# Degree sums on GpSimd, counts turned by DMA in the second gate layer, and a last product in halves, in a four-layer graph network on one core

## The reference, cut to what matters

```python
# layer 0: x1 = x @ W1 + b1, then four gate layers, on the edge list of a fixed graph (row, col)
deg = segment_sum(ones, col);  dis = maximum(deg, 1.0) ** (-0.5)
alpha = tanh(x_i @ gw[:512] + x_j @ gw[512:] + gb)
gnn_out = gnn_out + segment_sum(dis[row] * dis[col] * alpha * x_j, col)
# layer 1: two mean layers
mean = segment_sum(h[src], dst) / maximum(deg, 1.0)
h = h @ W_self + mean @ W_neigh + b
# layer 2: attention, summed over src instead of dst
e = exp(-leaky_relu(al[src] + ar[dst]));  h_prime = segment_sum(e * h[dst], src) / (rowsum + 1e-5)
# layer 3: GCN
out = relu(segment_sum((x @ W)[src] * dinv[src] * dinv[dst], dst) + b)
x = layernorm(x + out)
```

## Time and profile before

| what | us |
|---|---|
| median of 3 runs | 1544.73 (1543.46 to 1545.18) |
| profiled execution | 1543.31, its span 1541.5 |
| PE busy | 1516.2 (98%) |
| DVE busy | 880.5 (57%) |
| ACT busy | 751.4 (49%) |
| POOL busy | 189.9 (12%) |
| granted TensorE clock | 0.998 |

### The profile page before, as it was taken

One profiled execution on the slowest core, in us unless ns is written; L12 is line 12 of the kernel. 1 busy time (PEld: TensorE's weight loads), 2 busy tenths in 40 slices (PEclk: granted clock), 3 DMA queues, 4 the chain that ended last, 5 costly groups with the idle time before them and its releaser, 6 DMA issues.

```text
span 1541.5 us, 19211 instructions
## 1 busy us (share of the span) xinstructions
PE 1516.2 (98%) x6965; PEld 1217.6 (79%) x6965; DVE 880.5 (57%) x1401; ACT 751.4 (49%) x1358; POOL 189.9 (12%) x315
## 2 busy tenths in 40 slices
PE   7999999999999999999999999999999999999997
PEld 5877877878887888788878777888788778877775
DVE  8878888887645353322333344567598356435346
ACT  7567677768733332334332133335696246533232
POOL 1110021324200000000000000212053013100013
PEclk9999999999999999999999999999999999999999
DMA  5333153325774434433344424564466248545245
GB/s 193 118 111 123 34 185 131 101 83 191 262 258 145 155 107 134 141 100 134 114 167 128 147 80 155 193 215 162 149 193 192 94 143 295 183 131 171 91 126 180
DMA packets 103198, 231.75 MB, mean 150 GB/s; under 512 B 23162, under 2 KB 25972, under 8 KB 103096
## 3 DMA queue, kind: packets, MB, share of 16 engines
q1 hardware_dynamic: 89996, 191.54, 39.1%
q10 hardware_dynamic: 13100, 38.86, 6.5%
HBM read 170.98 MB, written 59.37 MB: 149 GB/s over the span
## 4 chain that ended last, share of the span: by engine, by line
PE 92%; DVE 4%; ACT 3%; issue 1%; DMA 0%; POOL 0%; DVEq 0%; POOLq 0%; ACTq 0%
PE bank L980 17%; PE bank L836 15%; PE bank L838 15%; PE bank L837 15%; PE bank L991 9%; PE bank L984 8%; PE bank L982 7%; PE bank L1044 2%; ACT Tt L1125 2%; PE bank L906 1%; DVE Tt L1433 1%; PE bank L874 1%; DVE oK L1708 1%; DVE Zl L1474 0%; ACT Zh L1159 0%
## 5 line engine op out<-in xcount | busy, mean ns | idle before, releaser
L836 PE MATMUL bank<-wh,xh 128*125 128x512 f32 x1032 | 415.3, 402 | 0.4 <-issue 0.4
L837 PE MATMUL bank<-wl,xh 128*125 128x512 f32 x1040 | 410.4, 395 | 0.0
L838 PE MATMUL bank<-wh,xl 128*125 128x512 f32 x1040 | 409.5, 394 | 0.0
L980 PE MATMUL bank<-Zh,Mh 125*125 125x512 f32 x1000 | 399.6, 400 | 1.0 <-ACT Mh L1107 1.0
L1407 DVE TENSOR_TENSOR xl<-xs,xh 128x1000 fp32r<-128x1000 f32 x130 | 155.4, 1198 | 291.5 <-ACT xh L1090 291.2
L1090 ACT CAST xh<-xs 128x1000 fp32r<-128x1000 f32 x130 | 132.9, 1026 | 304.5 <-PE bank L838 292.9
L991 PE MATMUL bank<-Zl,Mh 125*125 125x512 f32 x600 | 236.6, 394 | 0.0
L838 PEld LDWEIGHTS bank<-wh,xl 128*125 128x125 f32 x1040 | 193.0, 186 | 48.9
L837 PEld LDWEIGHTS bank<-wl,xh 128*125 128x125 f32 x1040 | 193.1, 186 | 44.4
L836 PEld LDWEIGHTS bank<-wh,xh 128*125 128x125 f32 x1032 | 191.1, 185 | 45.2 <-issue 0.7
L980 PEld LDWEIGHTS bank<-Zh,Mh 125*125 125x125 f32 x1000 | 185.4, 185 | 46.2 <-ACT Mh L1107 1.1
(11 more groups left out here) (171 smaller groups left out, 1811.7 us busy)
## 6 DMA issues: line engine op xcount, KB each, us to landing
xs<-xT_d SPq DMA_DIRECT2D x80, 500.0 KB, 3.6
Ar<-a_d SPq DMA_DIRECT2D x100, 312.5 KB, 3.3
xs<-hT_d SPq DMA_DIRECT2D x40, 500.0 KB, 3.5
x_d<-XO ACTq DMA_DIRECT2D x30, 512.0 KB, 4.9
R<-x_d SPq DMA_DIRECT2D x60, 256.0 KB, 4.3
xT_d<-XT ACTq DMA_DIRECT2D x30, 500.0 KB, 3.5
ws<-in_W SPq DMA_DIRECT2D x30, 256.0 KB, 3.7
...
```

The lines of the kernel that those rows point to most:

```text
L836: te.matmul(o, xh[i % 2][:, k, :], wh[s][:], start=(k == 0), stop=False)
L837: te.matmul(o, xh[i % 2][:, k, :], wl[s][:], start=False, stop=False)
L838: m = te.matmul(o, xl[i % 2][:, k, :], wh[s][:], start=False, stop=(k == 7))
L980: te.matmul(o, Mh[i][:, s, :], zh, start=(n == 0), stop=False)
```

## The change

1. The 100 transposes, ACT's 30 copies of them and the ten early stores of at_d go. The tiles of counts get 128 columns a block (`ArF`, `AF16`, a_d, at_d), with three columns of zeros.
2. The degrees come from `sums` on GpSimd: three additions a tile (625, 250 and 125 elements a partition, from Af to a new tile AS), and from `degree` on PE: two products by a column of ones, 14 chunks after a tile is complete. For tile 9 they stand after seven of the eight pieces of the ninth x1 product. DVE copies the sums from PSUM.
3. In the second gate layer SP transposes each Ar tile by DMA into TT (`turn`) and stores it to at_d (`store_turned`).
4. The zeros of A16 are set by DVE, no longer by GpSimd.
5. The last product is made in two halves of 256 columns in two banks (`last_product`, 40 matmuls), and DVE works on the first half while PE makes the second (`last_post`). GpSimd makes only the root (`pow`), and DVE the Newton step and the shift. The statistics of the left half, which were taken in the last ten jobs, are taken in the ten before them.

```diff
+DEGREE_AT = [C_LAST[3 * b + 2] + 14 for b in range(NT - 1)]
...
-        ArF = [sb(f"Ar{i}", [128, NT, T], i16) for i in range(2)]
-        Ar = [t[0:T, :, :] for t in ArF]
+        ArF = [sb(f"Ar{i}", [128, NT, 128], i16) for i in range(2)]
+        Ar = [t[0:T, :, 0:T] for t in ArF]
+        TT = [sb(f"TT{i}", [128, NT, 128], i16) for i in range(2)]
...
+                if NT <= i - 2 < 2 * NT:
+                    q.wait_ge(d_turn[i % 2], 16 * ((i - 2 - NT) // 2 + 1))
...
                 sy.dma_start(ArF[i % 2][:], src).then_inc(d_ar[i % 2], 16)
+                if NT <= i - 1 < 2 * NT:
+                    turn(i - 1)
+                if NT <= i - 2 < 2 * NT:
+                    store_turned(i - 2)
+
+            def turn(i):
+
+                b = i - NT
+                q.wait_ge(d_ar[i % 2], 16 * (i // 2 + 1))
+                q.wait_ge(d_at[b % 2], 16 * (b // 2))
+                sy.dma_start_transpose(TT[b % 2][:], ArF[i % 2][:].rearrange("p a c -> p (a c)")).then_inc(d_turn[b % 2], 16)
+
+            def store_turned(i):
+                b = i - NT
+                q.wait_ge(d_turn[b % 2], 16 * (b // 2 + 1))
+                sy.dma_start(at_d[b], TT[b % 2][:]).then_inc(d_at[b % 2], 16)
...
-                for k in range(u, w):
-                    m = te.transpose(bank[6 + i % 2][0:T, (k - u) * T:(k - u + 1) * T], Af[b % 2][:, k, :],
-                                     ident[0:T, 0:T])
-                m.then_inc(s_tt, 1)
+            def degree(t):
+
+                q.wait_ge(s_as, t + 1)
+                if t == 5:
+                    q.wait_ge(s_deg, 1)
+                for n in range(2):
+                    m = te.matmul(bank[7][0:T, t:t + 1], AS[t % 2][:, n, :], ones[0:T, 0:1], start=(n == 0), stop=(n == 1))
+                m.then_inc(s_dp, 1)
...
-                        for b in range(NT - 1):
-                            for n in range(3):
-                                if c == C_LAST[3 * b + 2] + 4 + 2 * n:
-                                    at_part(b, n)
+                        if c in DEGREE_AT:
+                            degree(DEGREE_AT.index(c))
...
-                for k in range(4):
+                for k in range(7):
                     x_part(8, k)
-                for n in range(3):
-                    at_part(NT - 1, n)
-                for k in range(4, 8):
-                    x_part(8, k)
+                degree(NT - 1)
+                x_part(8, 7)
...
+            def last_product():
...
+                for n, (u, w) in enumerate(PARTS):
+                    o = bank[LAST_BANKS[n]][0:T, u:w]
+                    for s in range(NT):
+                        zh, zl = z_tile(z + s)
+                        te.matmul(o, Mh[i][:, s, :], zh[:, u:w], start=(s == 0), stop=False)
...
+                        m = te.matmul(o, Mh[i][:, s, :], zl[:, u:w], start=False, stop=(s == NT - 1))
+                    m.then_inc(s_part, 1)
...
-                    q.wait_ge(s_tt, i + 1)
-                    if t >= 2 and n == 0:
-                        q.wait_ge(d_at[t % 2], 16 * (t // 2))
-                    q.wait_ge(s_pad, 4)
-                    ac.activation(AT16[t % 2][0:T, u:w, :], bank[6 + i % 2][0:T, 0:(w - u) * T]
-                                  .rearrange("p (a c) -> p a c", c=T), ACT.Copy, accum_out=DEG3[:, t, n:n + 1]).then_inc(s_te, 1)
...
+                for n, (a, b) in enumerate(PARTS):
+                    p = bank[LAST_BANKS[n]][0:T, :]
+                    q.wait_ge(s_part, n + 1)
+                    chain("v", ve.scalar_tensor_tensor(u[:, a:b], p[:, a:b], D3[:, d:d + 1], B[0:T, a:b], ALU.mult, ALU.add))
+                    mine()
+                    chain("v", ve.scalar_tensor_tensor(R[r % 4][:, a:b], u[:, a:b], 0.0, R[r % 4][:, a:b], ALU.max, ALU.add))
+                    mine()
+                    chain("v", ve.bn_stats(st4[:, 2 + n, :], R[r % 4][:, a:b]))
...
+                q.wait_ge(s_root, 1)
+                mine()
+                chain("v", ve.tensor_scalar(m[:, 4:5], m[:, 3:4], m[:, 3:4], m[:, 4:5], ALU.mult, ALU.mult))
+                mine()
+                chain("v", ve.tensor_scalar(m[:, 3:4], m[:, 4:5], 1.5, m[:, 3:4], ALU.add, ALU.mult))
+                mine()
+                ve.tensor_scalar(m[:, 5:6], m[:, 0:1], m[:, 3:4], -1.0, ALU.mult, ALU.mult).then_inc(s_rstd, 1)
...
+                for i, t in enumerate(AF16):
+                    ve.memset(t[96:128, :, :], 0.0).then_inc(s_pad, 1)
+                    q.wait_ge(s_pad, 2 * i + 1)
+                    ve.memset(t[:, :, T:128], 0.0).then_inc(s_pad, 1)
...
+                if j == NJ - 1:
+                    po.tensor_tensor(m[:, 3:4], m[:, 2:3], half[0:T, 0:1], ALU.pow).then_inc(s_root, 1)
+                    return
...
+            def sums(t):
+
+                q.wait_ge(s_ev, 3 * t + 3)
+                if t >= 2:
+                    q.wait_ge(s_dp, t - 1)
+                o, a = AS[t % 2], Af[t % 2]
+                chain("p", po.tensor_tensor(o[:], a[:, 0:5, :], a[:, 5:10, :], ALU.add))
+                mine()
+                chain("p", po.tensor_tensor(o[:, 0:2, :], o[:, 0:2, :], o[:, 2:4, :], ALU.add))
+                mine()
+                po.tensor_tensor(o[:, 0, :], o[:, 0, :], o[:, 4, :], ALU.add).then_inc(s_as, 1)
...
-            for i, t in enumerate(AF16 + AT16):
-                po.memset(t[96:128, :, :], 0.0).then_inc(s_pad, 1)
-                q.wait_ge(s_pad, i + 1)
-            rsqrt_degrees(0, 5, 1)
+            for t in range(NT):
+                sums(t)
+                if t == 6:
+                    rsqrt_degrees(0, 5, 1)
             rsqrt_degrees(5, NT, 3)
```

121 lines of the change are left out of this document (75 added, 46 removed).

## The result

The changed kernel takes 1546.88 us (median of 20 runs, 1544.69 to 1550.96), the kernel before 1544.72 us (20 runs, 1542.72 to 1546.11). The ratio is 1.0019, with a 95% interval of 1.0013 to 1.0025: it is slower, by 2 to 4 us. The forecast was 1557 in a range of 1541 to 1566, slower with a chance of 0.81. The direction was right, the size was not: +12.3 us was forecast and +2.2 came.

The account below looks back on a forecast made before the run. PE was taken to bound the kernel, with VectorE some 10% behind in the loop. Terms 13.8 - 0.5 + 0.3 + 0.5 - 1.5 = +12.6 on 1543.3 us profiled gave 1555.9, and 1557 as median; range 1541 to 1566.

Parts of the forecast that it names:

- The bound passes to VectorE: Chunk loop: PE sets the pace before; after, PE waits for VectorE throughout, some 20 us for oK; loop 108.4 us, +13.8.
- PE's gain: Count stage: dropping transposes for degree products saves PE 7.4 us, 6.7 in the loop, useful only if VectorE can follow.
- oK is held: Chunk loop: GpSimd's additions also block the one-input operation oK, raising its mean from 313 to about 375 ns.
- Rivals 1 and 2: Chunk loop: first, only two-input operations held, not oK, 1540 us, 13%; second, no hold or one in idle time, 1535, 3%.
- The size of the hold: Chunk loop: three additions hold VectorE for their whole 2.70 us a tile, less 7%, nine tiles: 22.6 us.
- L1679, left out at -0.8: Start: this VectorE operation is no longer held 0.8 us by GpSimd's memset; possible -0.8 us, not counted in the sum.
- From the loop to the first gate job, -0.5: Stretch between loop and first gate job: 12.5 us instead of 13.0, including 0.9 us waiting for tile 9's sums.
- Second gate layer, +0.5: Transposing DMA taken at 5 us, over within a job; GpSimd's additions move: +0.5 us (-1 to +3).
- Rival 3: Second gate layer: the transpose outlasts a job, so each load waits for it; 1578 us at 10.2 us each, 11%.
- The end, -1.5: End of kernel: half-width operations before the root -0.8, VectorE replacing GpSimd behind it -0.8, product halves +0.1: -1.5 us (-2.2 to 0).
- rival 1: Chunk loop: GpSimd's additions exclude only two-input operations, loop -3.4, 1540 us, 13%; turning point a hold of about 1.1 us a tile.
- My own case: Whole kernel: oK is held and VectorE bounds the loop; 1557 us, from 1550 to 1565 by its terms' bounds, 73%.

Follow-up runs that it names:

- The stretch by itself: Changed kernel with a separate stretch ahead, VectorE operations beside GpSimd's additions and fills; only the stretch read: oK held 1.04, 0.37 and 0.16 us, 1.57 a tile.
- e_two_zeros: Kernel before with the last product in halves and two of the four zero fills on VectorE: 1542.75 us, ratio 0.9988.
- e_no_turn: Changed kernel without the turning transfer and the store of its result, attention loading the counts as they are: 1546.64 us, ratio 1.0013.

## Why the prediction was right or wrong

**The bound passes to VectorE: right.** The earlier trace rows gave PE as the bound with VectorE 10% behind. After the change VectorE has 95.5 of 100.2 us, and PE waits for oK, 12.4 us where some 20 were forecast.

**PE's gain: right.** With everything but the additions in place the loop's last oK came 7.3 us earlier than before (93.43 instead of 100.77). Of these 1.3 are the start, and the remaining 6.0 stand beside the 6.7 us forecast.

**oK is held: right.** The mean of 370 ns is close to the forecast (375), and single oKs take 1.34 us. Rivals 1 and 2, no hold of oK or none at all, fall with it.

**The size of the hold: this is the step that failed.** The term was 9 x 2.70 x 0.93 = 22.6 us. The 2.70 took whole durations for holds, and one of them, 783 ns, was itself a duration with a wait in it. The stretch by itself shows 0.41 us for the third addition and a hold that is shorter than the duration by 0.26 us for each of the three: 2.70 - 0.37 - 3 x 0.26 = 1.55, measured 1.57. With this in the same formula the term is 9 x 1.57 x 0.93 = 13.1 us, the loop 85.1 - 0.6 + 13.1 + 1.3 = 98.9, and the change of the loop +4.3 us; the three profiles show +5.5 to +6.0. VectorE's busy time from the first oK to the last rose by 11.6 us (82.9 to 94.5, mean of three), which is the term's true size, half of the 22.6. A second miss went the other way: the formula took away all 9.5 us of VectorE's waits, and its idle time fell only from 9.0 to 3.2 us. The two measured parts, +11.6 and -5.8, make the +5.8 of the loop. Rows to see the first miss by were at hand. In the earlier trace rows L1592 ended at 1132.05 + 1.59 = 1133.64, so that its own 0.69 us began at 1132.95, and the addition ended at 1133.09: the hold stopped 0.14 us before that end. I passed over it as "until GpSimd was through". In the earlier trace rows L1679 ended at 7.00 us with 0.25 us of its own, so that it began at 6.75, 0.15 us before the memset's end, and I called that "the whole rest of the memset". And the check by oK's mean could not tell 13 from 23 us, because most of the excess had been put on other operations.

**L1679, left out at -0.8: it was worth 1.1 us.** The operation takes 0.24 us instead of 1.05, and the edges' work starts 0.3 us sooner. The first oK comes at 7.8 instead of 8.9, and e_two_zeros shows that most of it, 0.8 us, is still there at the first gate job.

**From the loop to the first gate job, -0.5: -0.8.** From the end of the last oK it was 15.7 us before and is 14.9 in all three profiles. Tile 9's products wait 0.90 us for `sums`, as forecast (0.9).

```profile
113.21 0.59 PE L894 MATMUL bank<-ones,AS 125*125 125x1 f32 x4 [0.90 <-POOL AS L1998]
```

**Second gate layer, +0.5: 0, or a little less.** The transposing transfer was bounded at 2.9 to 10.2 us and taken at 5. The list of DMA issues (KB where known, us to landing) has a median of 4.4, the slowest of the ten took 6.8, and e_no_turn gives it no price that can be told. From its first `times` to that of the next layer the second gate layer takes 56.5 to 56.6 us in the three profiles, where it was 58.3 (58.5 in the one of e_no_turn); the three others are 1.7 us longer together. Rival 3 falls, and with it the estimate of 13.1 us from the Trainium skill's figure for one block. The statement of the Trainium skill, "Advanced Engine Details and Errata", section "X-Bar Transpose (TRN2)", that such transfers are as fast as others, comes close: the plain load of the same bytes takes 3.7.

```profile
Ar<-a_d SPq DMA_DIRECT2D x100, 320.0 KB, 3.7
...
TT<-Ar SPq DMA_TRANSPOSE x10, 4.4
```

`times` in that layer takes 1.46 us at 229.36 where it took 2.20 in the earlier trace rows: GpSimd's additions have moved off it, as the prediction thought possible.

**The end, -1.5: -1.3.** The three operations on 256 columns take 0.48, 0.42 and 0.43 us, 0.26 to 0.27 less than the full ones (0.75, then 0.69 and 0.69), where 0.27 was taken. From the root's start to ACT's start it is 1.61 us instead of 2.21, a gain of 0.6 where 0.8 was taken.

```profile
1537.79 0.77 POOL L1982 TENSOR_TENSOR mv<-mv,half 125x1 f32<-125x1 f32 x1 [1.57 <-DVE mv L1564]
...
1539.40 0.81 ACT L1259 ACTIVATE G<-G,mv 125x512 f32<-125x512 f32 x1 [2.33 <-DVE mv L1574]
```

**The sum, with what was measured (means of three profiles):** loop +5.8, start -1.2, from the last oK to the gate job -0.8, and the rest -1.0 make +2.8 in the spans, where +12.6 had been forecast; the medians differ by 1.8 to 2.2. Of the miss of 9.8 us the loop has 8.0, the start 1.2, the way to the gate job 0.3 and the rest 0.3. The turning point was named: a hold of 1.1 us a tile in rival 1. The 1.3 us by which VectorE's busy time grew for each of nine tiles lie 0.2 above it, nine times some 2 us, and that is about the loss. The range held the time, but by luck: its lower end came from rival 1. My own case ended at 1550, because the bounds of the loop's term (+11 and +18) varied the discount and the handing over, and not the hold itself.
